# Transposing rotated queries and keys by DMA in place of TensorE, in a fused cross-attention and gene-FFN kernel

## The reference, cut to what matters

```python
q = (layernorm(x) @ Wq).reshape(b, n, 32, 16)
k, v = split(ctx @ Wkv);  k, v as (b, 128, 32, 16)
q, k = rope(q, pos), rope(k, pos)                 # x1*cos - x2*sin, x1*sin + x2*cos
w = softmax(einsum('bqhd,bkhd->bhqk', q, k) / 4)
x = x + einsum('bhqk,bkhd->bqhd', w, v).reshape(b, n, 512) @ Wout + bout
y = layernorm(x);  xn = y * rsqrt(mean(y*y) + eps) * norm_w
top, idx = top_k(xn @ Wc.T / clip(temperature, 0.1), 32)
e = einsum('btk,btkc->btc', softmax(top), genes[idx])
out = x + tanh(e @ Wd.T) * xn * (e @ Wu.T) * scale
```

## Time and profile before

| | |
|---|---|
| median of three runs | 611.38 us (610.16, 611.38, 612.52) |
| span of the profiled execution | 611.7 us |
| its mean granted TensorE clock | 0.954 of full speed |
| TensorE matmuls | 501.1 us busy, 82% |
| VectorE | 442.2 us, 72% |
| ScalarE | 308.3 us, 50% |
| GpSimd | 221.3 us, 36% |
| DMA | 17.61 MB, mean 29 GB/s |

### The profile page before, as it was taken

One profiled execution on the slowest core, in us unless ns is written; L12 is line 12 of the kernel. 1 busy time (PEld: TensorE's weight loads), 2 busy tenths in 40 slices (PEclk: granted clock), 3 DMA queues, 4 the chain that ended last, 5 costly groups with the idle time before them and its releaser, 6 DMA issues.

```text
span 611.7 us, 12095 instructions
## 1 busy us (share of the span) xinstructions
PE 501.1 (82%) x4378; PEld 371.0 (61%) x4378; DVE 442.2 (72%) x740; ACT 308.3 (50%) x450; POOL 221.3 (36%) x231
## 2 busy tenths in 40 slices
PE   0076787898989899898989898989898999968644
PEld 0064565666767666666667676667676676745533
DVE  2358067788888787887878878888887876858381
ACT  0464545565564737382837465655647374805021
POOL 0063435343534434262624453435334356200000
PEclk9997699999999999999999999999999999969676
DMA  7900000001010100000010101010100000000000
GB/s 254 261 0 10 20 10 20 10 2 44 3 44 1 34 10 32 12 17 27 0 43 1 43 1 43 1 43 1 43 1 17 10 17 2 19 2 2 17 18 17
DMA packets 16149, 17.61 MB, mean 29 GB/s; under 512 B 7536, under 2 KB 9600, under 8 KB 16128
## 3 DMA queue, kind: packets, MB, share of 16 engines
q1 hardware_dynamic: 10304, 13.92, 7.2%
q10 hardware_dynamic: 5824, 3.41, 2.1%
HBM read 12.86 MB, written 4.19 MB: 28 GB/s over the span
## 4 chain that ended last, share of the span: by engine, by line
PE 56%; DVE 25%; issue 9%; ACT 5%; ACTq 4%; DVEq 1%; POOLq 0%; POOL 0%
PE gene L1125 18%; DVE row_max L824 10%; PE dense L1125 8%; PE dense L1240 6%; PE gene L1297 5%; PE gene L1290 3%; ACTq L451 3%; PE score_b L1249 3%; PE dense L1187 3%; ACT qT L539 2%; PE gene L1307 2%; PE gene L1308 2%; DVE neg_max L836 2%; DVE yn L877 2%; DVE bn L865 2%
## 5 line engine op out<-in xcount | busy, mean ns | idle before, releaser
L903 DVE MAX8 top<-stage_b 128x8 f32<-128x1024 f32 x64 | 78.6, 1228 | 49.3 <-ACT stage_b L579 44.9
L353 POOL TENSOR_TENSOR stage_b<-stage_b,cos_t 128x512 f32<-128x512 f32 x32 | 41.3, 1290 | 162.1 <-issue 152.5
L911 DVE MATCH_REPLACE8 stage_b<-top,stage_b 128x1024 f32<-128x1024 f32 x64 | 77.5, 1211 | 0.2
L1125 PE MATMUL gene<-wcT_h,yT_h 128*128 128x512 f32 x128 | 55.0, 430 | 1.5 <-DVE yT_l L882 1.5
L388 POOL TENSOR_TENSOR x_ring<-x_ring,down 128x512 f32 (+1 forms) x16 | 20.4, 1272 | 97.8 <-DVE down L952 97.8
L1125 PE MATMUL gene<-wcT_h,yT_l 128*128 128x512 f32 x128 | 52.3, 408 | 0.0
L1125 PE MATMUL gene<-wcT_l,yT_h 128*128 128x512 f32 x128 | 52.0, 407 | 0.0
L374 POOL TENSOR_TENSOR parts<-turned,parts 128x512 f16<-128x512 f32 x32 | 37.6, 1176 | 20.5 <-issue 19.5
L1240 PE MATMUL dense<-stage_a,v_ext 128*32 128x128 f32 x1024 | 39.4, 282 | 4.7 <-ACT stage_a L553 4.6
L824 DVE TENSOR_REDUCE row_max<-score_a 128x8 f32<-128x1024 f32 x32 | 39.0, 1220 | 4.0 <-issue 3.1
L579 ACT ACTIVATE stage_b<-gene 128x512 f32<-128x512 f32 x32 | 19.1, 596 | 43.9 <-PE gene L1125 43.9
(11 more groups left out here) (157 smaller groups left out, 1228.9 us busy)
## 6 DMA issues: line engine op xcount, KB each, us to landing
x_ring<-x_dram SPq DMA_DIRECT2D x16, 256.0 KB, 2.7
out_dram<-x_ring SPq DMA_DIRECT2D x16, 256.0 KB, 2.0
ctx_sb<-ctx_dram SPq DMA_DIRECT2D x16, 128.0 KB, 2.1
stage_a<-L_ffn_Wc_dram SPq DMA_DIRECT2D x1, 2048.0 KB, 18.7
stage_b<-L_xattn_Wq_dram ACTq DMA_DIRECT2D x1, 1024.0 KB, 5.9
stage_b<-L_xattn_Wkv_dram SPq DMA_DIRECT2D x1, 1024.0 KB, 10.1
stage_b<-L_xattn_Wout_dram ACTq DMA_DIRECT2D x1, 1024.0 KB, 15.1
qT<-neg_maxT SPq DMA_DIRECT2D x64, 4.0 KB, 1.7
```

The costliest lines, as they stand in the source:

```text
L353: pool.tensor_tensor(halves(qk_cos), halves(qk_sb), trig(cos_t, t), ALU.mult).then_inc(s_cosm[n], 1)
L903: nc.vector.max(top[:, 8 * n:8 * n + 8], logit if n == 0 else rest).then_inc(s_top[n], 1)
L911: nc.vector.match_replace(rest, top[:, 8 * n:8 * n + 8], logit if n == 0 else rest, REMOVED).then_inc(s_rem[n], 1)
L1125: last = nc.tensor.matmul(out, lhs[:, k * P:(k + 1) * P], rhs(k), start=(n == 0), stop=(n == steps - 1))
```

## The change

The 32 TensorE transposes of a tile and the four ScalarE copies behind them are gone, with `pair_in`, `transpose_qk`, `read_qkT` and the semaphores `s_tr` and `s_trr`. In their place SP issues two transposing DMAs per tile, one from the key parts to `kT`, one from the query parts to `qT`, each of 128 x 2048 f16 (512 KB) as 16 blocks of 128 x 128. They stand behind `shift` and ahead of the store, keys first. The keys' rope sum and split move ahead of the queries' rope on GpSimd, and their high part ahead of `read_q` on ScalarE. `project_v` now stands ahead of `project_out`.

```diff
+            def turn(t, n):
+
+                hold(sp)
+                sp.wait_ge(s_hi[n], t + 1)
+                sp.wait_ge(s_lo[n], t + 1)
+                if not first(t):
+                    sp.wait_ge(s_st[3], t)
+                sp.dma_start_transpose((qT, kT)[n][:].rearrange("p (m t) -> p m t", t=P),
+                                       (q_parts, k_parts)[n].rearrange("p h l d -> p (h l d)")).then_inc(s_turned[n], 16)
+
             def iteration(l, a, b, c, d):
...
                 if b is not None:
                     shift(b)
+                if a is not None:
+                    turn(a, 1)
+                    turn(a, 0)
                 if d is not None:
                     store(d)
...
                 if not first(t):
-                    pool.wait_ge(s_tr[2 * n + 1], t)
+                    pool.wait_ge(s_turned[n], 16 * t)
                 to = (q_parts[:, :, 1], k_parts[:, :, 2])[n]
...
                     rope(a, 1)
+                    rope_sum(a, 1)
+                    split_lo(a, 1)
                     rope(a, 0)
                     rope_sum(a, 0)
-                    rope_sum(a, 1)
                     split_lo(a, 0)
-                    split_lo(a, 1)
...
             def split_hi(t, n):
                 act.wait_ge(s_rot[n], t + 1)
                 if not first(t):
-                    act.wait_ge(s_tr[2 * n + 1], t)
+                    act.wait_ge(s_turned[n], 16 * t)
...
                     read_logits(c, 1)
                 if a is not None:
+                    split_hi(a, 1)
                     read_q(a)
...
                     split_hi(a, 0)
                 if b is not None:
                     read_oT(b, 1)
-                if a is not None:
-                    split_hi(a, 1)
                 if d is not None:
                     tanh(d)
-                if a is not None:
-                    read_qkT(a, 0)
-                    read_qkT(a, 1)
                 if b is not None:
                     attn_hi(b)
-                if a is not None:
-                    read_qkT(a, 2)
                 if c is not None:
                     gene_exp(c)
                 if a is not None:
-                    read_qkT(a, 3)
                     read_v(a)
...
             def scores(t, g):
                 if g == 0:
-                    for n in range(4):
-                        pe.wait_ge(s_trr[n], t + 1)
+                    for n in range(2):
+                        pe.wait_ge(s_turned[n], 16 * (t + 1))
...
                 if b is not None:
                     transpose_o(b)
-                if a is not None:
-                    transpose_qk(a, 0)
-                    transpose_qk(a, 1)
                 if b is not None:
                     transpose_attn(b)
                 if a is not None:
-                    transpose_qk(a, 2)
-                    transpose_qk(a, 3)
+                    project_v(a)
                 if b is not None:
                     project_out(b)
-                if a is not None:
-                    project_v(a)
```

More of the change, by code:

```diff
@@ L160, in build @@
         s_xb = sem("bout_added")
-        s_tr = [sem(f"qkT{n}_in_psum") for n in range(4)]
-        s_trr = [sem(f"qkT{n}_read") for n in range(4)]
+        s_turned = [sem(f"{x}T_turned") for x in "qk"]
         s_sc = [sem(f"scores{g}_in_psum") for g in range(GROUPS)]
@@ L530, in split_hi @@
                                      ACT.Copy).then_inc(s_hi[n], 1)
-            def read_qkT(t, n):
-                act.wait_ge(s_tr[n], t + 1)
-                if not first(t):
-                    act.wait_ge(s_st[3], t)
-                dst = (qT, qT, kT, kT)[n][:, (n % 2) * 1024:(n % 2 + 1) * 1024]
-                src = dense[:, (n % 2) * 512:(n % 2 + 1) * 512].bitcast(f16)
-                nc.scalar.activation(dst, src, ACT.Copy).then_inc(s_trr[n], 1)
             def read_neg_max(t):
@@ L1134, in transpose_x @@
                 pe.wait_ge(s_xn, t + 1)
-                if not first(t):
-                    pe.wait_ge(s_trr[2], t)
+                if isinstance(t, int) and t == 1:
+                    pe.wait_ge(s_q_sb, 1)
+                elif not first(t):
+                    pe.wait_ge(s_oT[0], t - 1)
                 for k in range(XK):
@@ L1142, in transpose_ctx @@
                 pe.wait_ge(s_ctx, (t + 1) * 16)
-                if not first(t):
-                    pe.wait_ge(s_trr[3], t)
+                if isinstance(t, int) and t == 1:
+                    pe.wait_ge(s_k_sb, 1)
+                elif not first(t):
+                    pe.wait_ge(s_oT[1], t - 1)
                 for k in range(CK):
@@ L1166, in project_v @@
                            CK).then_inc(s_v, 1)
-            def transpose_qk(t, n):
-                if n == 0:
-                    pe.wait_ge(s_hi[0], t + 1)
-                    pe.wait_ge(s_lo[0], t + 1)
-                    pe.wait_ge(s_q_sb, t + 1)
-                    if not first(t):
-                        pe.wait_ge(s_oT[0], t)
-                elif n == 1:
-                    pe.wait_ge(s_k_sb, t + 1)
-                    if not first(t):
-                        pe.wait_ge(s_oT[1], t)
-                else:
-                    if n == 2:
-                        pe.wait_ge(s_hi[1], t + 1)
-                        pe.wait_ge(s_lo[1], t + 1)
-                    pe.wait_ge(s_trr[n - 2], t + 1)
-                half = dense[:, (n % 2) * 512:(n % 2 + 1) * 512].bitcast(f16)
-                for m in range(8):
-                    last = nc.tensor.transpose(half[:, m * P:(m + 1) * P],
-                                               pair_in(n // 2, (n % 2) * 8 + m), ident16[:])
-                last.then_inc(s_tr[n], 1)
             def scores(t, g):
                 if g == 0:
-                    for n in range(4):
-                        pe.wait_ge(s_trr[n], t + 1)
+                    for n in range(2):
+                        pe.wait_ge(s_turned[n], 16 * (t + 1))
                     if not first(t):
@@ L1409, in draining @@
                     values(b, 2)
-                if a is not None:
-                    transpose_qk(a, 0)
-                if b is not None:
                     values(b, 3)
@@ L1443, in begin @@
                 duT()
-                for n in range(4):
-                    transpose_qk(0, n)
                 pe.wait_ge(s_genes, 32)
```

14 lines of the change are left out of this document (removed).

## The result

The changed kernel takes **615.27 us** (median of 10 runs, 612.75 to 618.04); the kernel before, on the same chip, 610.74 (10 runs, 609.42 to 612.52). The ratio is 1.0077, with a 95% interval of 1.0057 to 1.0096: slower by 4.5 us, where 608.5, 2.9 faster, had been forecast. The profiled execution took 616.06 us, its span is 614.3 (before: 611.7), and its mean granted TensorE clock is 0.924 (before: 0.954). The two spans differ by less than the medians, because the profiled execution of the kernel before is one of its slower ones: beside experiment 9 its executions with a clock of 0.954 to 0.956 have spans of 609.4 to 612.0 us, those with 0.961 have 607.2 to 609.3.

A forecast was written before the change was run, and what follows sets the result against it. Bound: the chain of waits, 32.53 us per iteration, mostly on TensorE, crossing to VectorE. 14 x (-0.44 + 0.10) = -4.8, tile 0 +1.9, last tile 0: -2.9, giving 608.5 us; range 603 to 730.

The forecast's parts named there:

- Part 2: Two transposing DMAs per tile: 5.0 us each (3.7 to 6.2), queries' landing 3.5 us early, 0 cost in the loop.
- The pieces of 256 B: Each transposing DMA moves as 2048 pieces, 128 per engine at 35 ns, plus 1.7 us to land: 6.2 us.
- Rival 2: Transposing DMAs run slowly, block by block, 9.6 us of issue each; queries' land 7.4 us late: 730 us, chance 0.17.
- the forecast's own 603 to 614: Range of the forecast's own case for the whole kernel; 614 with DMAs of 6.2 us and a late last tile.
- Rival 2's slowest case: Each transposing DMA takes 27 us, as 16 full landings: about 1220 us in all, left outside the stated range.
- Part 1: Without transposes and copies, project_v ahead of project_out: its inputs are ready earlier, gaining 0.44 us per tile for 14 tiles.
- part 4: Keys' steps moved earlier: GpSimd sums delay VectorE's mask to x_lo, L838 keeps its place, +0.10 us per tile.
- Part 3: Tile 0: its two transposing DMAs end at 54.3, where scores had started at 52.40: +1.9 us.
- rival 1: GpSimd's first keys' sum gets in before VectorE's L838 (negate_max): 0.66 us later per tile, 616 us, chance 0.25.
- rival 1's sign: negate_max's L838 on VectorE at 0.8 us or more, where 0.19 us speaks for the forecast.

The follow-up runs named there:

- experiment 9: The kernel before with only project_v moved ahead of project_out, all 32 transposes still on TensorE: 632.87 us, ratio 1.0327.
- Experiment 12: Changed kernel with useless matmuls in two gaps and keys' rope held until maxima are negated, plus queries' DMA held until aT_l is written: 602.81 us (593.88 without that).
- experiment 1: Changed kernel plus eight useless matmuls per iteration in TensorE's gap ahead of the third score group: 606.77 us, ratio 0.9929 to the kernel before.
- experiment 3: Changed kernel with GpSimd's keys' rope held until negate_max of the same iteration is done: 614.53 us, ratio 1.0069 to the kernel before.
- experiment 2: Changed kernel plus four useless matmuls per iteration in TensorE's gap ahead of the third score group: 608.98 us, ratio 0.9971 to the kernel before.
- experiment 10: Changed kernel with queries' transposes back on TensorE, only keys by DMA, project_v behind project_out: 610.90 us; with keys' rope held until maxima are negated, 600.58 us.

## Why the prediction was wrong

**Part 2, the DMAs: right.** They land in 4.3 us (median of 16 each) where 5.0 was taken between 3.7 and 6.2. From the time line of SP's queue, changed kernel:

```profile
331.72 1.83 SPq L306 DMA_TRANSPOSE kT<-parts  x1
336.29 1.71 SPq L306 DMA_TRANSPOSE qT<-parts  x1
```

The queries' land at about 340.6 and the scores start at 343.67: 3.1 us ahead of need, where 3.5 was said. The pieces of 256 B were right as well: the first queue has 76864 packets instead of 10304, 2080 more for each of the 32 DMAs. Its share rose from 7.2% to 21.3%, which makes 21 ns for a packet and not 35, and 130 of them on each engine with 1.7 us to land give 4.4 us. Experiment 12 shows the cover by removing it. Rival 2 (730 us) is out, and with it the upper part of the range. The stated range of 603 to 730 holds 615.27 only because it was stretched to that rival; the forecast's own 603 to 614 does not. (Rival 2's slowest case, 27 us each, was given as about 1220; with the 46 us of tile 0, which that figure leaves out, it is about 1260. Nothing hangs on it.)

**Part 1: the term of 0.44 us was right, the sentence behind it was the error.** `attn_hi` starts at the end of the transposes and V follows without a gap:

```profile
338.58 0.65 PE L1221 MATMUL gene<-ident,attn 128*128 128x128 f32 x4 [1.18 <-DVE attn L831]
338.99 0.48 PE L1108 MATMUL score_b<-wkv_h,cT_h 128*128 128x512 f32 x1
...
339.27 0.60 ACT L564 ACTIVATE aT_h<-gene 128x512 fp32r<-128x512 f32 x1 [3.03 <-PE gene L1221]
...
339.90 0.69 DVE L837 TENSOR_TENSOR aT_l<-gene,aT_h 128x512 fp32r<-128x512 f32 x1
...
340.70 0.47 PE L1108 MATMUL gene<-wout_h,aT_h 128*128 128x512 f32 x1
```

`project_out` starts 0.11 us behind `attn_lo`'s end, and with the gap filled a period is 32.02 against 32.53: 0.51 gained where 0.44 was forecast (0.34 with part 4). The step that failed is: "More is not to be had: TensorE could start `scores` some 1.9 us earlier than 309.37, since V is out of its way, but the first row maximum ... waits for the norm". That is true, and I took the 1.9 us as worth nothing. They are an idle gap, worth less than nothing: 0.45 us of waiting became 2.38, the granted clock fell to 0.56 for 3.4 us, `project_k` took up to 1.3 us more, and the tile lost 1.0 us (experiment 1). In the profiled executions the stretch from the first to the last `normalise` is 484.7 us before, 477.8 with the gap filled and 487.5 as changed: 6.9 gained, 9.7 lost again.

**Part 3.** Tile 0 was to cost 1.9 us. Its DMAs were issued at 44.45 and 46.71, but its first scores waited for VectorE's `wduT_l` and began at 52.30, against 52.40 in the earlier trace rows: no cost from the DMAs. `normalise` of tile 0 is 0.33 us later.

**Part 4 and rival 1.** With the clock up, L821 kept its place (0.19 us in all but the first iteration of experiment 1), as the forecast said. In the changed kernel it took 1.2 us in 11 of 16, rival 1's sign, but not by rival 1's mechanism: not the *sum* got in ahead but the sine product, since the maxima came late. The Trainium skill, page "SBUF — State Buffer", section "SBUF: two separate sides", states the exclusive lock on the port pair that GpSimd and VectorE share; the trace agrees again, with 0.19 against 1.20 us. Of the two times that the prediction gives for L838 and L923, the 0.94 us is L836's and the 1.20 us L838's. L923, which is L906 with the change, takes 1.22 us in the earlier trace rows and mostly 1.77 in experiment 1, where the sums get in its way as part 4 foresaw. Rival 1's time, 616, is near the result by luck: against the kernel with the gap filled, the late row maxima cost 0.80 us and the negation only 0.26, and experiment 3 took the whole wait for the port away and gained 0.7 us.

**The chances.** Slower had 0.37, the largest of the three, but none of it for the reason that held; no rival named TensorE's clock.

What stays open: why the clock falls in some iterations with the same gap and not in others (11 iterations of the changed kernel have a slow `project_k`, 4 have not; the gap of 1.18 us was followed by the lower clock once each in experiments 1 and 2, four times in experiment 3), and why it is every fourth in experiment 10 and every third in its version with the wait.

## What to carry to other kernels

When work is taken off TensorE, or moved, ask where the freed time will lie. If the chain around the loop runs over another engine at that point, it becomes an idle gap, and the matmuls behind the gap may run at half the clock; look at the granted clock of each stretch, not only at busy time. Leave independent work standing where TensorE must wait, put other work there, or as a test fill the gap with useless matmuls: if the time falls although work was only added, the idle time behind it was costing clock.

## What the runs showed of the hardware that was not expected

- Gaps of 2.4 us behind a busy stretch, pairs of 1.2 and 1.5 us, and in experiments 1 to 3 a gap of 1.2 us with none of over 0.6 us in the 6 us before it, were followed by the lower clock; where it was read by stretch, it was 0.55 to 0.56 over the next 3 to 5 us; matmuls of 512 columns then take 0.63 us instead of 0.40 (they overlap, so six take 2.9 instead of 1.64). With a 0.5 us gap in the same place it stayed at 1.00. With 1.45 us in that place it fell in 4 of 15 iterations.
- Eight useless matmuls per iteration made a kernel faster by 8.5 us of 615.
- A transposing DMA of 128 x 2048 f16 from SBUF to SBUF took 4.3 us from issue to landing (4.3 to 5.0 for the keys'), 1.3 to 2.0 us of it on the issuing queue in the loop.
- A wait that holds GpSimd's rope back made the kernel before 8 us faster, since VectorE's negation then takes 0.18 us instead of 0.93.
